# A transformer layer on eight cores: the layer norm's two stages and the attention's softmax closing in another order

## The chip, the cores and the metric

The kernel runs on one Trainium2 chip, on all 8 cores, each with one sequence of the batch (2048 tokens of 2048 features); the cores exchange nothing. The metric is the time of the slowest core in microseconds, as the median of several executions. TensorE is called PE, its weight loads PEld, VectorE DVE, ScalarE ACT, GpSimd POOL and SyncE SP, as in the profile.

## What is computed

The reference, cut to what matters, for the x of one core:

```python
def _layernorm(x, eps=1e-5):
    m = mean(x); v = var(x)
    return (x - m) / sqrt(v + eps)

# attention: 16 heads of 128
q, k, v = ln(x) @ wq, ln(x) @ wk, ln(x) @ wv
q, k = rope(q) / sqrt(128), rope(k)
probs = softmax(where(causal, q @ k.T, -1e30))
x = x + (probs @ v) @ wo

# experts: all 8 are computed, the gate keeps 2 per token, and 1 shared expert of twice the width
h = ln(x)
w = top2(softmax(h @ gate_w.T)), normalised
y = sum over experts e of w[e] * (silu(h @ w1[e]) * (h @ w3[e])) @ w2[e]
x = x + y + (silu(h @ sw1) * (h @ sw3)) @ sw2
```

## The kernel before

The program is one list of instructions per engine, written by a small class: `emit` appends an instruction to the list of its engine, with the semaphore values that it has to wait for and the semaphore that it raises. Each engine runs its list strictly in the order in which the Python code emitted it, so the order of the emitting lines is the order of the work. The stages follow one another and most begin behind a barrier:

1. First layer norm (lines 290 to 354), 16 tiles of 128 tokens. For each tile, SP loads 128x2048 float32 values of x into one of three buffers `xt`. `emit_ln` computes the statistics on ACT: a Copy whose accumulator gives the sum (line 292), and then a Square whose accumulator gives the sum of squares (line 295). Four tiny DVE instructions follow (mean, mean of squares plus eps, square of the mean, variance; lines 298 to 303), then Ln and Exp on ACT for the inverse root (lines 304 and 306), and the normalisation on DVE (line 308) into one of two bfloat16 buffers `sqb`. `emit_transposes` then turns the tile by 16 PE transposes into four groups of PSUM and copies the groups out on ACT (line 340). In the same stretch a long POOL DMA loads the whole of wk.
2. Projections of k, q and v with rope (lines 362 to 477), spilled to DRAM.
3. Attention (lines 530 to 642), 16 heads, each in two epochs of 1024 queries: the first epoch has 12 pieces of up to 512 queries against 128 keys, the second 28. For each piece PE makes the scores (line 575, into a PSUM slot), ACT takes the exponential (line 582), DVE masks it where the piece lies on the diagonal (line 589), and PE multiplies it twice: by a column of ones for the softmax sums Z (line 601, weights 128x1, into row 0 of the lower half of PSUM tensor `pB`) and by v for the output (line 609). The two multiplications come LA = 2 steps behind the scores. There are four score slots: two in the lower half of `pA`, and two in that upper half of `pA` or `pB` which the epoch's output does not use. When all pieces of an epoch are through, the epoch is closed: ACT copies Z out of PSUM (`zsb`, line 617), takes Ln and Exp(-x) of it (lines 620 and 622), PE spreads the reciprocal over 128 partitions by two matmuls with one row of weights (line 626), into the half that held slots 2 and 3, ACT copies that out (`bcs`, line 632), and DVE multiplies the output by it (`ATTNT`, line 636).
4. Output projection with the residual (lines 644 to 699).
5. Second layer norm with the gate (lines 708 to 796). The tile's layer norm is that of stage 1. 16 small matmuls (line 783) then give the gate's logits, which ACT copies out (line 790), and `gate_chain` (lines 725 to 768) computes the two weights per token: five tiny DVE instructions, two ACT exponentials (lines 737 and 740), seven more DVE instructions, one PE transpose (line 756), a DVE copy (line 761) and an SP store of the weights. `gate_chain` of a tile is emitted just ahead of the next tile's `emit_ln`.
6. The experts' first matrices (lines 840 to 910), with a spread of the next expert's gate weights at each expert's last block (`emit_gate_bcast`, line 831).
7. The experts' second matrices and the output (lines 925 to 1008).

What decides when a score may be written:

```python
sslot = step % 4
if sslot < 2: sps, soff, sw = pA, sslot * 512, [piece_free[sslot]]
else:         sps, soff, sw = bcps, 1024 + (sslot - 2) * 512, [piece_free[sslot], attn_free]
```

Of the kernel before, what the change touches and what calls it, by code (L numbers as in the profile page):

```python
# [10 lines left out]
AF = mybir.ActivationFunctionType  # L11
# [111 lines left out]
def build(taps=(), upto="p5b"):  # L123
# [126 lines left out]
    with contextlib.ExitStack() as stack:  # L250
# [40 lines left out]
        def emit_ln(xtile, dstb, src_toks, sq_waits=()):  # L291
            tcp = emit("scalar", lambda e: e.activation(dstb[:, :], xtile[:, :], AF.Copy,  # L292
                                                        accum_out=STATS[:, 0:1]),
                       waits=list(src_toks) + list(sq_waits), inc="s_s")
# [3 lines left out]
            vchain(lambda e: e.tensor_scalar_mul(STATS[:, 2:3], STATS[:, 0:1], 1.0 / D),  # L298
                   extra=[tsq])
            vchain(lambda e: e.tensor_scalar(STATS[:, 3:4], STATS[:, 1:2], 1.0 / D, EPS,  # L300
                                             ALU.mult, ALU.add))
            vchain(lambda e: e.tensor_mul(STATS[:, 4:5], STATS[:, 2:3], STATS[:, 2:3]))
            tv = vchain(lambda e: e.tensor_sub(STATS[:, 6:7], STATS[:, 3:4], STATS[:, 4:5]))
            tln = emit("scalar", lambda e: e.activation(STATS[:, 7:8], STATS[:, 6:7], AF.Ln),
                       waits=[tv], inc="s_s")
            tr = emit("scalar", lambda e: e.activation(STATS[:, 8:9], STATS[:, 7:8], AF.Exp,
                                                       scale=-0.5), waits=[tln], inc="s_s")
            emit("vector", lambda e: e.tensor_scalar(dstb[:, :], xtile[:, :], STATS[:, 2:3],  # L308
                                                     STATS[:, 8:9], ALU.subtract, ALU.mult),
# [38 lines left out]
        sq_free = [None, None]  # L348
        for i in range(NT):
# [180 lines left out]
        piece_free = {0: None, 1: None, 2: None, 3: None}  # L530
# [7 lines left out]
        for n in range(NH):  # L538
# [102 lines left out]
            if n + 2 < NH:  # L641
                hload[n + 2] = load_head(n + 2, [p.tokt("s_t")])
# [430 lines left out]
```

How the kernel before makes its waits and increments, by code:

```python
                def _(eng):  # L104
                    for fn, waits, incs in oplist:
                        for (s, v) in waits:
                            if v > 0 and lastwait.get(s, -1) < v:
                                eng.wait_ge(semh[s], v)
                                lastwait[s] = v
                        inst = fn(eng)
                        if inst is None:
                            assert not incs
                            continue
                        for (s, amt) in incs:
                            r = inst.then_inc(semh[s], amt)
                            if r is not None:
                                inst = r
```

## Time and profile before

| what | us |
|---|---|
| median of 4 timed executions | 7399.71 |
| the four: lowest, second, third, highest | 7374.02, 7380.34, 7419.08, 8093.21 |
| the profiled execution, its own time | 7080.52 |
| the profiled core's span (core 0, the slowest) | 7079.0 |
| spans of the eight cores | 7012.4 to 7079.0 |
| PE busy | 6255.1 (88%) |
| DVE busy | 1145.3 (16%) |
| ACT busy | 1048.2 (15%) |

| stage on core 0 | from | to |
|---|---|---|
| first layer norm | 0 | 186 |
| projections | 194 | 1018 |
| attention | 1037 | about 1800 |
| output projection | about 1800 | 2231 |
| second layer norm and gate | 2233 | 2450 |
| experts, first matrices | 2454 | about 5640 |
| experts, second matrices | about 5640 | 7079 |

The profile is one execution on the slowest core. A row of the timeline has the start and the duration, the engine, the line of the code, the operation, what is written from what, and in brackets how long the engine had been idle before it and what released it. "PEclk" is the share of TensorE's full clock that was granted. An engine that waits is not slow: what counts in a stage is which engine's chain the others wait for.

### The profile page before, as it was taken

Reading aid. Unit: us, or ns where it says so; the run is one execution under the profiler, and the core shown is the slowest. Engines: PE = TensorE matmul, PEld = TensorE weight load, DVE = VectorE, ACT = ScalarE, POOL = GpSimd, SP = SyncE. Lnnn points to the kernel's source line nnn. Section 1 sums busy time; section 2 is a strip of 40 time slices with the busy share of each in tenths; the row PEclk is TensorE's granted clock in tenths of the full one; section 3 lists DMA queues with packets and bytes.
Section 4 is the critical chain, followed back from the end, with each engine's and each line's share of the span. In section 5 each row is a group of like instructions: output and inputs, shape, how many; then the busy total and the mean of one; then the engine's idle time right before and its main releaser. Section 6 shows DMA issues by size and latency. Waiting matters only on the chain.

```text
span 7079.0 us, 66124 instructions; the slowest of 8 cores (7012.4 to 7079.0 us)
## 1 busy us (share of the span) xinstructions
PE 6255.1 (88%) x28144; PEld 2693.2 (38%) x28144; DVE 1145.3 (16%) x1337; ACT 1048.2 (15%) x1305; POOL 305.9 (4%) x280
## 2 busy tenths in 40 slices
PE   1778887777664399999999999999999999999999
PEld 1333331111222144444444444444444444444444
DVE  1222101111111211111111111111000122222222
ACT  5100116666101400000000000000000000000000
POOL 0000000000000000000000000000000000000000
PEclk9999997777887599999999999999999999999999
DMA  5133131010444144444444444444454544574544
GB/s 143 34 79 58 45 72 36 27 36 27 85 91 102 60 54 56 61 54 56 56 59 54 54 63 54 54 58 59 54 74 54 141 109 116 119 189 124 126 107 130
DMA packets 738001, 536.17 MB, mean 76 GB/s; under 512 B 531232, under 2 KB 652192, under 8 KB 733616
## 3 DMA queue, kind: packets, MB, share of 16 engines
q0 software_dynamic: 530896, 207.83, 25.4%
q1 hardware_dynamic: 92896, 208.76, 9.5%
q10 hardware_dynamic: 113920, 115.35, 5.1%
q8 instruction: 227, 3.72, 0.2%
q14 instruction: 62, 0.51, 0.0%
HBM read 623.18 MB, written 116.46 MB: 104 GB/s over the span
## 4 chain that ended last, share of the span: by engine, by line
PE 83%; DMA 7%; ACT 5%; DVE 3%; issue 2%; SPq 0%; DVEq 0%; ACTq 0%; POOL 0%; POOLq 0%
PE pB L879 22%; PE pA L864 21%; PE pA L975 11%; PE pB L975 10%; DMA xq<-xin 5%; PE pA L383 3%; PE pB L383 3%; PE pB L601 3%; PE pB L609 2%; PE pA L575 2%; PE pA L463 2%; PE pB L463 2%; DVE t2b L407 1%; ACT sqb L295 1%; ACT sqb L292 1%
## 5 line engine op out<-in xcount | busy, mean ns | idle before, releaser
L879 PE MATMUL pB<-XLNT,w3c 128*128 128x512 bf16 x7040 | 1555.1, 382 | 0.0
L864 PE MATMUL pA<-XLNT,w1c 128*128 128x512 bf16 x7040 | 1539.6, 379 | 2.1 <-ACT beb L837 2.1
L879 PEld LDWEIGHTS pB<-XLNT,w3c 128*128 128x128 bf16 x7040 | 692.1, 98 | 848.4 <-issue 29.0
L864 PEld LDWEIGHTS pA<-XLNT,w1c 128*128 128x128 bf16 x7040 | 689.8, 98 | 834.5 <-issue 6.0
L975 PE MATMUL pA<-w2s,aslg 128*128 128x512 bf16 x3520 | 788.6, 380 | 7.7 <-DMA AT_sp<-afin 5.3
L975 PE MATMUL pB<-w2s,aslg 128*128 128x512 bf16 x3520 | 785.8, 379 | 0.0
L871 ACT ACTIVATE silu<-pA 128x2048 bf16<-128x2048 f32 x110 | 206.5, 1877 | 2824.2 <-PE pA L864 2772.1
L892 DVE TENSOR_TENSOR atmp<-silu,pB 128x2048 bf16<-128x2048 bf16 x88 | 201.3, 2288 | 2165.2 <-PE pB L879 2140.9
L975 PEld LDWEIGHTS pA<-w2s,aslg 128*128 128x128 bf16 x3520 | 344.8, 98 | 426.0 <-issue 13.3
L975 PEld LDWEIGHTS pB<-w2s,aslg 128*128 128x128 bf16 x3520 | 344.4, 98 | 415.3
L582 ACT ACTIVATE exp<-pA,EXB 128x512 bf16<-128x512 f32 (+3 forms) x544 | 340.9, 640 | 146.9 <-PE pA L575 142.5
L677 PE MATMUL pA<-woq,ATTNT 128*128 128x512 bf16 x768 | 206.4, 432 | 110.8 <-DVE x2q L684 110.8
L575 PE MATMUL pA<-qtn,ktn 128*128 128x512 bf16 (+3 forms) x544 | 219.3, 415 | 48.7 <-DVE ATTNT L636 26.9
L994 DVE TENSOR_TENSOR Yacc<-Yacc,pB 128x1024 f32<-128x1024 f32 x144 | 175.9, 1222 | 508.9 <-PE pB L975 493.4
L994 DVE TENSOR_TENSOR Yacc<-Yacc,pA 128x1024 f32<-128x1024 f32 x144 | 175.9, 1222 | 508.2 <-PE pA L975 504.3
L329 PE MATMUL pA<-IDB,sqb 128*128 128x128 bf16 x256 | 32.4, 306 | 245.2 <-DVE sqb L308 245.2
L601 PE MATMUL pB<-exp,ONESC 128*1 128x512 bf16 (+3 forms) x640 | 239.7, 375 | 2.2 <-DVE exp L589 0.5
L518 POOL DMA_DIRECT2D w1c<-w x88 | 100.8, 1145 | 2231.1 <-PE pA L864 2231.1
L589 DVE TENSOR_TENSOR exp<-exp,TRIUB 128x128 bf16<-128x128 bf16 x256 | 57.6, 225 | 712.2 <-ACT exp L582 712.2
L609 PE MATMUL pB<-exp,vn 128*128 128x512 bf16 (+1 forms) x448 | 172.5, 385 | 0.0
L677 PEld LDWEIGHTS pA<-woq,ATTNT 128*128 128x128 bf16 x768 | 80.5, 108 | 236.5 <-issue 175.3
L383 PE MATMUL pA<-XLNT,qc 128*128 128x512 bf16 x512 | 120.5, 399 | 43.0 <-DMA qc<-wq 24.4
(119 smaller groups left out, 2721.9 us busy)
## 6 DMA issues: line engine op xcount, KB each, us to landing
aslg<-AT_sp ACTq DMA_DIRECT2D x80, 1408.0 KB, 8.2
AT_sp<-afin SPq DMA_DIRECT2D x110, 512.0 KB, 7.9
w1c<-w POOLq DMA_DIRECT2D x88, 512.0 KB, 6.7
w3c<-w POOLq DMA_DIRECT2D x88, 512.0 KB, 10.8
w2s<-w POOLq DMA_DIRECT2D x16, 2816.0 KB, 22.9
xt<-xin SPq DMA_DIRECT2D x16, 1024.0 KB, 8.3
xq<-xin SPq DMA_DIRECT2D x64, 256.0 KB, 5.1
X_sp<-x2q SPq DMA_DIRECT2D x64, 256.0 KB, 3.8
```

Of the source, the lines that this page charges most:

```text
L383: lhs_tile=lhs_tile: e.matmul(ps[:, c * 512:(c + 1) * 512], lhs_tile[:, lcol:lcol + 128], XLNT[:, db * 2048 + c * 512: db * 2048 + (c + 1) ...
L463: emit("tensor", lambda e, db=db, c=c, ps=ps, i=i: e.matmul(ps[:, c * 512:(c + 1) * 512], XLNT[:, db * 2048 + i * 128: db * 2048 + (i + 1) ...
L575: sps=sps, soff=soff: e.matmul(sps[:, soff:soff + b - a], ktn[par][:, j * 128:(j + 1) * 128], qtn[par][:, q0 + a:q0 + b], start=True, stop ...
L582: sps=sps, soff=soff: e.activation(expt[my_epar][:, 0:b - a], sps[:, soff:soff + b - a], AF.Exp, bias=EXB[:, 0:1]),
L601: stz=first_z[bank], gsp=grp_stop: e.matmul(pB[0:1, a:b], ONESC[:, :], expt[my_epar][:, 0:b - a], start=stz, stop=gsp),
L609: gsp=grp_stop, atps=atps: e.matmul(atps[:, 1024 + a:1024 + b], vn[par][:, j * 128:(j + 1) * 128], expt[my_epar][:, 0:b - a], start=stt, s ...
L677: emit("tensor", lambda e, nb=nb, i=i, pcol=pcol, wbuf=wbuf: e.matmul(pA[:, pcol:pcol + 512], ATTNT[:, nb * 2048 + i * 128: nb * 2048 + (i ...
L864: emit("tensor", lambda e, db=db, c=c, slot=slot: e.matmul(pA[:, c * 512:(c + 1) * 512], w1c[slot][:, db * 128:(db + 1) * 128], XLNT[:, db ...
L871: tsilu = emit("scalar", lambda e: e.activation(silu[:, :], pA[:, :], AF.Silu), waits=[th, silu_free], inc="s_s")
L879: emit("tensor", lambda e, db=db, c=c, slot=slot: e.matmul(pB[:, c * 512:(c + 1) * 512], w3c[slot][:, db * 128:(db + 1) * 128], XLNT[:, db ...
L975: ap2=cur_ap2, psl=psl: e.matmul(psl[0][:, psl[1] + c * 512: psl[1] + (c + 1) * 512], aslg[ap2][:, ib * 512 + kk * 128: ib * 512 + (kk + 1 ...
L994: tac = emit("vector", lambda e, k=k, psl=psl: e.tensor_add(Yacc[k][:, :], Yacc[k][:, :], psl[0][:, psl[1]:psl[1] + 1024]), waits=[tmm, ya ...
```

## The change

Three things are edited.

The layer norm is cut into `ln_stats` and `ln_rest`. The sum is now a `reduce_sum` on DVE over the float32 tile, the Copy on ACT is gone, and the Square stays on ACT. Statistics of tile i are emitted behind all the work of tile i-1 (its `ln_rest`, its transposes and its copies out), and `ln_rest` of tile i comes in the next turn of the loop. Two sets of columns of `STATS` alternate. The loads are emitted two tiles ahead. Both layer norms use this; in the second one, `gate_chain` of tile i-1 is now emitted behind the statistics of tile i and ahead of its `ln_rest`.

In the attention, the closing of an epoch is moved into `emit_zchain`, which is emitted at the start of the next epoch. The copy `zsb` is gone: Ln reads Z from PSUM itself. The scores have two slots, both in `pA`, and the two multiplications come LA = 3 steps behind.

```diff
+        def ln_stats(xtile, dstb, src_toks, sq_waits, C):
+            tsq = emit("scalar", lambda e: e.activation(dstb[:, :], xtile[:, :], AF.Square,
+                                                        accum_out=c1(C[1])),
                        waits=list(src_toks) + list(sq_waits), inc="s_s")
-            tsq = emit("scalar", lambda e: e.activation(dstb[:, :], xtile[:, :], AF.Square,
-                                                        accum_out=STATS[:, 1:2]),
-                       waits=[tcp], inc="s_s")
...
+            tsum = vchain(lambda e: e.reduce_sum(c1(C[0]), xtile[:, :], axis=AX.X),
+                          extra=list(src_toks))
+            return tsq, tsum
+
+        def ln_rest(xtile, dstb, tsq, tsum, C):
+            vchain(lambda e: e.tensor_scalar_mul(c1(C[2]), c1(C[0]), 1.0 / D),
+                   extra=[tsum])
+            vchain(lambda e: e.tensor_scalar(c1(C[3]), c1(C[1]), 1.0 / D, EPS,
+                                             ALU.mult, ALU.add), extra=[tsq])
...
+        def ln_finish(pend):
+            nonlocal ev_prev
+            j, jpar, jbpar, jst = pend
+            tx = ln_rest(xt[jpar], sqb[jbpar], *jst, LNCOLS[j % 2])
+            xt_free[jpar] = tx
+            ev_prev, sq_free[jbpar] = emit_transposes(j, ev_prev, tx, sqb[jbpar])
+
+        lts_q = {0: load_xt(0, 0, xin), 1: load_xt(1, 1, xin)}
         for i in range(NT):
             par = i % 3
             bpar = i % 2
-            lts = load_xt(i, par, xin)
-            tx = emit_ln(xt[par], sqb[bpar], lts, sq_waits=[sq_free[bpar]])
-            xt_free[par] = tx
-            ev_prev, sq_free[bpar] = emit_transposes(i, ev_prev, tx, sqb[bpar])
+            if pend_ln is not None:
+                ln_finish(pend_ln)
+            if i + 2 < NT:
+                lts_q[i + 2] = load_xt(i + 2, (i + 2) % 3, xin)
+            st = ln_stats(xt[par], sqb[bpar], lts_q[i], [sq_free[bpar]], LNCOLS[i % 2])
+            pend_ln = (i, par, bpar, st)
+        ln_finish(pend_ln)
...
+        LA = 3
+
+        def emit_zchain(st):
...
+            tlnz = emit("scalar", lambda e: e.activation(recf[:, :], pB[0:1, 0:1024],
+                                                         AF.Ln),
+                        waits=[st["tlast"]], inc="s_s")
...
+                if pend_z is not None:
+                    emit_zchain(pend_z)
+                    pend_z = None
...
-                        sslot = step % 4
-                        if sslot < 2:
-                            sps, soff = pA, sslot * 512
-                            sw = [piece_free[sslot]]
-                        else:
-                            sps, soff = bcps, 1024 + (sslot - 2) * 512
-                            sw = [piece_free[sslot], attn_free]
+                        sslot = step % 2
+                        sps, soff = pA, sslot * 512
...
-                            waits=([bc_free] if first_attn[bank] else []),
+                            waits=([tbcs_done[(epoch + 1) % 2]]
+                                   if first_attn[bank] else []),
...
-                tz = emit("scalar", lambda e: e.activation(zsb[:, :], pB[0:1, 0:1024], AF.Copy),
-                          waits=[tlast], inc="s_s")
-                z_free = tz
-                tlnz = emit("scalar", lambda e: e.activation(recf[:, :], zsb[:, :], AF.Ln),
-                            waits=[tz], inc="s_s")
...
+        def p3b_finish(pend):
...
+            if pending is not None:
+                gate_chain(*pending)
+                pending = None
+            tx = ln_rest(xt[jpar], sqb[jbpar], *jst, LNCOLS[j % 2])
```

DVE's list in the second layer norm, before: a tile's normalisation (L308), then the gate chain of that tile (L727 to L761), then the first two small instructions of the next tile's statistics.

```order
L308 TENSOR_SCALAR sqb_54<-xt_51,STATS 128x2048 [waits s_s]
L727 TENSOR_REDUCE STATS<-STATS 128x1 [waits s_v,s_s]
...
L735 TENSOR_TENSOR STATS<-STATS 128x1 [waits s_v]
L742 TENSOR_SCALAR STATS<-STATS 128x2 [waits s_v,s_s]
...
L761 COPY gt_58<-pB 8x128 [waits s_t]
L298 TENSOR_SCALAR STATS<-STATS 128x1 [waits s_v,s_s]
L300 TENSOR_SCALAR STATS<-STATS 128x1 [waits s_v]
```

The same place after the change, from one tile's normalisation (L315) to the next: the sum (L300), the gate chain (L754 to L788) and the rest of the layer norm (L305 to L315).

```order
L315 TENSOR_SCALAR sqb_55<-xt_52,STATS 128x2048 [waits s_s]
L300 TENSOR_REDUCE STATS<-xt_53 128x1 [waits s_v,l_xt2]
L754 TENSOR_REDUCE STATS<-STATS 128x1 [waits s_v,s_s]
...
L762 TENSOR_TENSOR STATS<-STATS 128x1 [waits s_v]
L769 TENSOR_SCALAR STATS<-STATS 128x2 [waits s_v,s_s]
...
L788 COPY gt_58<-pB 8x128 [waits s_t,st_gsp]
L305 TENSOR_SCALAR STATS<-STATS 128x1 [waits s_v]
L307 TENSOR_SCALAR STATS<-STATS 128x1 [waits s_v]
```

The sum of the next tile has moved in ahead of the gate chain, and the four small instructions of the layer norm, whose first one waited for ACT, now stand behind it without such a wait.

PE's list at the boundary of two epochs, before: the last multiplication by v (L609), the two spreading matmuls (L626), the scores of the next epoch (L575), its Z (L601) and output (L609).

```order
L609 MATMUL pB<-exp_80,vn_75 128x128
L626 MATMUL pA<-recb,ONESR 128x512 [waits s_s]
L626 MATMUL pA<-recb,ONESR 128x512
L575 MATMUL pA<-qtn_72,ktn_74 128x512 [waits l_h1]
L575 MATMUL pA<-qtn_72,ktn_74 128x512
L575 MATMUL pB<-qtn_72,ktn_74 128x384 [waits s_v]
L601 MATMUL pB<-exp_77,ONESC 1x512 [waits s_v]
L609 MATMUL pA<-exp_77,vn_76 128x512 [waits s_s]
L575 MATMUL pB<-qtn_72,ktn_74 128x512
L601 MATMUL pB<-exp_78,ONESC 1x512 [waits s_s]
```

The same boundary after the change, with the lines 655 (times v), 573 (spread), 621 (scores) and 647 (Z):

```order
L655 MATMUL pB<-exp_80,vn_75 128x128
L573 MATMUL pA<-recb,ONESR 128x512 [waits l_h1,s_s]
L573 MATMUL pA<-recb,ONESR 128x512
L621 MATMUL pA<-qtn_72,ktn_74 128x512 x2
L621 MATMUL pA<-qtn_72,ktn_74 128x384 [waits s_s]
L621 MATMUL pA<-qtn_72,ktn_74 128x512 [waits s_s]
L647 MATMUL pB<-exp_77,ONESC 1x512 [waits s_v]
L655 MATMUL pA<-exp_77,vn_76 128x512
L621 MATMUL pA<-qtn_72,ktn_74 128x256 [waits s_s]
L647 MATMUL pB<-exp_78,ONESC 1x512
```

The two spreading matmuls keep their place between the epochs. The third score waits for ACT instead of DVE, a fourth score stands ahead of the first Z, and from then on the wait for ACT stands at each score where it stood at each Z.

## Rows read from the trace of the kernel before

**Rows 1.** Windows view: us, busy (count) of PE, PEld, DVE, ACT, POOL, PEclk, DMA.
```profile
1018.00:1797.00 779.00, 593.98 (x1982) 134.61 (x1982) 94.31 (x287) 517.84 (x766) 5.72 (x5) 0.78 0.16 39
```

**Rows 2.** Timeline, one tile of the first layer norm, up to the next tile's Copy.
```profile
33.38 1.94 ACT L292 ACTIVATE sqb<-xt 128x2048 bf16<-128x2048 f32 x1
...
35.51 1.91 ACT L295 ACTIVATE sqb<-xt 128x2048 bf16<-128x2048 f32 x1
...
37.61 0.15 DVE L298 TENSOR_SCALAR STATS<-STATS 128x1 f32<-128x1 f32 x1 [6.97 <-ACT sqb L295]
37.87 0.15 DVE L300 TENSOR_SCALAR STATS<-STATS 128x1 f32<-128x1 f32 x1
...
39.25 1.35 DVE L308 TENSOR_SCALAR sqb<-xt,STATS 128x2048 bf16<-128x2048 f32 x1 [0.70 <-ACT STATS L306]
...
43.45 1.94 ACT L292 ACTIVATE sqb<-xt 128x2048 bf16<-128x2048 f32 x1
```

**Rows 3.** Groups by line: DVE's slowest 128x2048 instruction, busy us, mean ns.
```profile
L407 DVE TENSOR_TENSOR t2b<-pA,SSINB 128x2048 bf16<-128x2048 f32 x16 | 36.7, 2292 | 199.2 <-PE pA L399 199.2
```

**Rows 4.** DMA view of 35 to 45 us: the load of x issued there, us to landing.
```profile
xt<-xin SPq DMA_DIRECT2D x1, 1024.0 KB, 11.1
```

**Rows 5.** Timeline, one boundary of two epochs of the attention.
```profile
1096.15 1.01 ACT L617 ACTIVATE zsb<-pB 1x1024 f32<-1x1024 f32 x1 [0.95 <-PE pA L609]
1097.26 1.05 ACT L620 ACTIVATE recf<-zsb 1x1024 f32<-1x1024 f32 x1
1098.40 1.05 ACT L622 ACTIVATE recb<-recf 1x1024 bf16<-1x1024 f32 x1
...
1099.60 1.01 PE L626 MATMUL pB<-recb,ONESR 1*128 1x512 bf16 x2 [3.55 <-ACT recb L622]
...
1100.54 1.03 PE L575 MATMUL pA<-qtn,ktn 128*128 128x512 bf16 x2
...
1101.68 1.26 ACT L582 ACTIVATE exp<-pA,EXB 128x512 bf16<-128x512 f32 x2
...
1103.26 0.58 PE L575 MATMUL pA<-qtn,ktn 128*128 128x512 bf16 x1 [1.68 <-DVE ATTNT L636]
```

**Rows 6.** Timeline, one step in the middle of an epoch.
```profile
1108.40 0.38 PE L575 MATMUL pA<-qtn,ktn 128*128 128x512 bf16 x1
...
1108.88 0.69 ACT L582 ACTIVATE exp<-pA,EXB 128x512 bf16<-128x512 f32 x1 [0.16 <-PE pA L575]
...
1109.25 0.38 PE L575 MATMUL pA<-qtn,ktn 128*128 128x512 bf16 x1
```

**Rows 7.** Windows view, granted clock behind the third score of Rows 5.
```profile
1103.30:1107.40 4.10, 4.10 (x9) 0.66 (x10) 0.00 (x0) 1.88 (x3) 0.00 (x0) 0.50 0.00 0
1107.50:1111.00 3.50, 3.50 (x14) 0.77 (x12) 0.00 (x0) 2.58 (x5) 0.00 (x0) 1.00 0.00 0
```

**Rows 8.** Timeline, second layer norm, from one copy of the logits to the next.
```profile
2249.24 0.17 ACT L790 COPY STATS<-pB 128x8 f32<-128x8 f32 x1 [0.91 <-PE pB L783]
...
2250.90 0.20 ACT L737 ACTIVATE STATS<-STATS 128x1 f32<-128x1 f32 x1 [1.50 <-DVE STATS L735]
...
2251.50 0.17 DVE L742 TENSOR_SCALAR STATS<-STATS 128x2 f32<-128x2 f32 x1 [0.69 <-ACT STATS L740]
...
2254.12 0.28 DVE L761 COPY gt<-pB 8x128 f32<-8x128 f32 x1 [0.62 <-PE pB L756]
...
2257.13 1.34 DVE L308 TENSOR_SCALAR sqb<-xt,STATS 128x2048 bf16<-128x2048 f32 x1 [0.70 <-ACT STATS L306]
...
2262.26 0.17 ACT L790 COPY STATS<-pB 128x8 f32<-128x8 f32 x1 [0.91 <-PE pB L783]
```

**Rows 9.** Timeline, experts' first matrices, the end of the first expert.
```profile
2736.52 13.98 PE L864 MATMUL pA<-XLNT,w1c 128*128 128x512 bf16 x64
...
2752.67 1.86 PE L831 MATMUL pA<-gr,ONESR 1*128 1x512 bf16 x4 [2.17 <-ACT silu L871]
...
2754.46 16.46 PE L879 MATMUL pB<-XLNT,w3c 128*128 128x512 bf16 x64
```

More of the change, by code:

```diff
@@ L768, in gate_chain @@
             gsp_toks.append(tsp)
+        def p3b_finish(pend):
+            nonlocal ev_prev, gate_free, pending
+            j, jpar, jbpar, jst = pend
+            if pending is not None:
+                gate_chain(*pending)
+                pending = None
+            tx = ln_rest(xt[jpar], sqb[jbpar], *jst, LNCOLS[j % 2])
+            xt_free[jpar] = tx
+            ev_prev, sq_free[jbpar] = emit_transposes(j, ev_prev, tx, sqb[jbpar])
+            tev_all = ev_prev[3]
+            for db in range(ND):
+                emit("tensor", lambda e, db=db, j=j: e.matmul(
+                    pB[:, 0:8],
+                    XLNT[:, db * 2048 + j * 128: db * 2048 + (j + 1) * 128],
+                    GWTB[:, db * 8:(db + 1) * 8],
+                    start=(db == 0), stop=(db == ND - 1)),
+                    waits=[tev_all, gate_free], inc="s_t")
+            tg = p.tokt("s_t")
+            tgl = emit("scalar", lambda e, jbpar=jbpar: e.copy(
+                STATS[:, 48 + 8 * jbpar: 56 + 8 * jbpar], pB[:, 0:8]),
+                waits=[tg, chain_done[jbpar]], inc="s_s")
+            gate_free = tgl
+            pending = (j, jbpar, tgl)
+        p.phase(BAR3)
+        lts_q = {0: load_xt(0, 0, X2_sp), 1: load_xt(1, 1, X2_sp)}
         for i in range(NT):
@@ L773, in build @@
             p.phase(BAR3)
-            lts = load_xt(i, par, X2_sp)
-            if pending is not None:
-                gate_chain(*pending)
-                pending = None
-            tx = emit_ln(xt[par], sqb[bpar], lts, sq_waits=[sq_free[bpar]])
-            xt_free[par] = tx
-            ev_prev, sq_free[bpar] = emit_transposes(i, ev_prev, tx, sqb[bpar])
-            tev_all = ev_prev[3]
-            for db in range(ND):
-                emit("tensor", lambda e, db=db, i=i: e.matmul(
-                    pB[:, 0:8],
-                    XLNT[:, db * 2048 + i * 128: db * 2048 + (i + 1) * 128],
-                    GWTB[:, db * 8:(db + 1) * 8],
-                    start=(db == 0), stop=(db == ND - 1)),
-                    waits=[tev_all, gate_free], inc="s_t")
-            tg = p.tokt("s_t")
-            tgl = emit("scalar", lambda e, bpar=bpar: e.copy(
-                STATS[:, 48 + 8 * bpar: 56 + 8 * bpar], pB[:, 0:8]),
-                waits=[tg, chain_done[bpar]], inc="s_s")
-            gate_free = tgl
-            pending = (i, bpar, tgl)
+            if pend_ln is not None:
+                p3b_finish(pend_ln)
+            if i + 2 < NT:
+                lts_q[i + 2] = load_xt(i + 2, (i + 2) % 3, X2_sp)
+            st = ln_stats(xt[par], sqb[bpar], lts_q[i], [sq_free[bpar]], LNCOLS[i % 2])
+            pend_ln = (i, par, bpar, st)
+        p3b_finish(pend_ln)
+        pend_ln = None
         gate_chain(*pending)
```

80 lines of the change are left out of this document (42 added, 38 removed).

## The prediction

> **What bounds the kernel now.** I read the busy times of the page first: PE is busy for 88% of the span, and the two expert stages, two thirds of it, are dense matmuls that the change does not touch. So I went to the stages that it does touch, with the windows view for their totals and the timeline for one period of each. In all three the reader is to see a chain over several engines in which PE or ACT waits in turn.
>
> In the first layer norm one tile takes 10.07 us, from Copy to Copy (33.38 to 43.45) [rows 2]. Copy and Square follow each other on ACT, DVE's small steps wait for them, the normalisation for those, the transposes for it, and the next Copy stands behind the copies out. Nothing overlaps between tiles. The load of x is no part of the chain: it landed in 11.1 us while the wk transfer ran [rows 4], with three buffers, thus two tiles ahead.
>
> In the attention PE is busy for 594 of 779 us at a mean clock of 0.78 [rows 1]. A full step takes 0.85 us, and ACT is idle 0.16 us in it, waiting for PE [rows 6]: PE's own order is the limit, not the exponential. The loss is at the 31 boundaries between epochs: PE stands 3.55 us until the reciprocal is there, and 1.68 us more ahead of the third score, which waits for DVE's ATTNT [rows 5]. Behind that the clock is at 0.50, the 1.2 GHz level, until 1107.4, and then at 1.00 [rows 7].
>
> In the second layer norm a tile takes 13.02 us, from one copy of the logits to the next (2249.24 to 2262.26) [rows 8]: the same chain plus the gate.
>
> **First layer norm.** Removed: the Copy with the sum, 33.38 to 35.51, so 2.13 us of ACT per tile [rows 2]. Added: one float32 reduction of 128x2048 on DVE, which the trace does not show. The nearest rows are the normalisation, the same tile read once by DVE, at 1.35 us [rows 2], and DVE's slowest instruction of that size, 2.29 us [rows 3]. I take 2.29, since a reduction is not faster than a plain pass. For its path that choice does not matter: it stands directly behind the normalisation of the tile before, which ends at 40.60, and would end by 42.9, while ACT is at the copies out and starts the Square only where the Copy started, at 43.45. Its cover goes if it takes more than about 4.5 us. The mean then is also ready before the Square, so 0.26 us (L298 to L300) leaves the path. New period: 10.07 - 2.13 - 0.26 = 7.68 us, 2.39 less; over the 15 tiles behind the first 35.9 us. The first tile has nothing ahead of it: its sum runs beside the Square, and instead of 4.23 us (33.38 to 37.61) it takes at most 2.29 plus a hop of 0.11, 1.8 less. Together 37.7 us. The loads keep their distance: tile i's is still released by the normalisation of tile i-3 and needed at that of i-1, two periods later, 15.4 us against 11.1. What is late next is what was late before, the barrier behind the last copy out and the load of the cosine tables; wk landed long before (80 us).
>
> **Attention.** Emitting the closing at the head of the next epoch moves nothing by itself: PE's list has the two spreading matmuls between the same neighbours as before, and no score of the next epoch ahead of them. So the boundary stays, only shorter. First, the copy zsb goes: 1097.26 - 1096.15 = 1.11 us [rows 5], in all 32 closings, 35.5 us. Ln has to read PSUM now; I cost that at nothing, as both kinds of 1x1024 ACT instruction take 1.01 to 1.05 us [rows 5]. Second, the third score has a slot in pA and waits for the first exponential instead of ATTNT. That exponential starts at 1101.68 and takes 0.69 [rows 6]; with the hop of 0.15 from ACT to PE (1098.40 + 1.05 to 1099.60) the score could start at 1102.52 instead of 1103.26, 0.74 earlier. The fourth score now stands ahead of the first Z and waits for the second exponential: both together end at 1101.68 + 1.26 = 1102.94, with the hop 1103.09. The third score occupies PE for 0.43 us at that clock (512 columns at 1.2 GHz), to 1102.95, so 0.14 of the gain goes again. Left: 0.60 us at 31 boundaries, 18.6 us. LA = 3 is costed at nothing: PE's amount of work is the same, and Z does not wait for exponentials in the middle of an epoch now.
>
> The new waits: each score waits for the exponential two steps back, where it was four. Behind that wait stand the Z and output matmuls of the step, and ACT waits for the score. A slot turns around in 0.48 (score to exponential, 1108.40 to 1108.88) + 0.69 + 0.15 = 1.32 us, against two steps of 0.85, 1.70 [rows 6]. The slack is 0.38 us: no cost. Attention together 54.1 us. Its bounds: the copy alone, with every microsecond of it worth half (below), 18, and 54 plus the clock's whole price, 131.
>
> **Second layer norm.** Here the order of DVE matters. Before, the gate chain of tile i-1 had its second half under the Copy and Square of tile i. Now it stands ahead of the small steps of tile i, and its two exponentials stand on ACT behind the Square. The new period, step by step, starting at the copy of the logits: 0.17 for it, then the Square 2.13 (as from one ACT pass to the next [rows 2]); during it the gate's first five DVE steps run, 1.66 us (2249.24 to 2250.90), hidden. Then the exponentials, 0.60 (2250.90 to 2251.50), the seven DVE steps, PE's transpose and DVE's copy, 2.62 (to 2254.12), that copy and a hop, 0.39, the small steps up to the normalisation, 1.64 (37.61 to 39.25 [rows 2]), and from there to the next copy of the logits 5.13 (2257.13 to 2262.26). Sum 12.68, against 13.02: the Copy's 2.1 us and the first half of the gate are bought with the second half of the gate. 0.34 over 15 tiles is 5.1, and 1.8 for the first tile as above: 6.9 us. Here the layer norm's stages gain alike in work and not at all alike in time. The bounds: 0, and 15 times 2.39 plus 1.8, so 38, if nothing of the gate came onto the path.
>
> **Sum.** 37.7 + 54.1 + 6.9 = 98.7 us. The span of 7079.0 becomes 6980, the profiled execution's 7080.5 becomes 6982. The timed median is 7399.7, 4.5% above the profiled execution, and the profile does not show why. The three stages are bound by fixed times of ACT, DVE and hops, so I subtract the same microseconds: 7301.
>
> **The rivals.**
>
> The slow clock keeps its end. Below the boundary PE works at half rate until 1107.4 [rows 7]. If that moment does not come earlier with PE's work, what is moved forward only fills the slow stretch and gains half: 1.71 / 2 at 31 boundaries plus 1.1, 28 us in place of 54. For it: the clock is granted by what PE does, and the first part of the gain is only an earlier start of four matmuls. Against: PE works without a gap for the 4.1 us before the clock is back, and that gapless work starts earlier by the whole 1.71. Total 73 us, 7327.
>
> The clock does not fall. PE's idle time shrinks from 3.55 to 2.44 us. A drop of the clock costs 16.46 - 13.98 = 2.48 us, as in the 64 matmuls behind the gate's spread [rows 9], so without it 31 times 2.48, 77 us more: 7224. Against: in that same place the idle time was only 2.17 us, shorter than the 2.44, and the clock fell.
> The Trainium skill, "TensorE: Matmul & The Clock Gate", section "Why this matters for your kernels", advises to keep the idle gaps between bursts of matmuls short, and its limit would let the shortened gap pass. By that rule this rival would be the forecast; the trace does not agree, with its fall behind 2.17 us, and I go by the trace.
>
> The loads of x hold the pace. Under the wk transfer they came every 10.07 us because nobody asked for more. If they cannot come faster there, the first 8 tiles gain nothing: 8 x 2.39 = 19 us less, 7320. Against: they landed in 11.1 us, and two are allowed to be under way.
>
> Slower: the two score slots. If PE's wait at each score also keeps it from loading the weights ahead, each of the 640 scores pays the hop of 0.15 and a weight load, 134.61 / 1982 = 0.07 us [rows 1]: 0.22 x 640 = 141 us, 42 more than all gains, 7442. It decides from 98.7 / 640 = 0.15 us per score. For it: the wait moves from Z, where it was, to the score, whose weights are loaded under the matmul before. Against: the slack of 0.38 us per pair of steps, so the wait is over when PE comes to it.
>
> The boundary stays as it is. If the closing took as long as before, because Ln from PSUM is slow by the microsecond of the copy, 35 us would go: 7337. The rows speak against it.
>
> **How the numbers follow.** Forecast 0.52, with a range of its own of 7285 to 7317. The clock keeping its end 0.19, the loads 0.08, the closing staying 0.05, the two slots 0.04, the clock not falling 0.05, and 0.07 for part of that gain at some boundaries (about 7270). The range reaches to the cases on both sides, and the timed runs themselves scatter by 20 us around their median: 7258 to 7356. One per cent is 74 us, about what a measurement of this kernel can tell from no change. Faster by over 1%: the forecast, the clock's two good cases and a little more than a fourth of the others, 0.71. Within 1%: 0.25. Slower: 0.04.
>
> **What would show it.** Right: a tile of the first layer norm in about 7.7 us with DVE's sum beginning at the normalisation's end and ending before the Square; ACT's Ln 0.3 us behind the last matmul of an epoch, PE idle about 2.4 us there and about 0.9 us ahead of the third score; steps of 0.85 us in the middle; two epochs together shorter by 2 x 1.71 = 3.4 us; a tile of the second layer norm in about 12.7 us with the gate's second half on DVE behind the Square. Wrong: a middle step longer than 0.85 us, with PE waiting for ACT at the scores; two epochs shorter by less than 2 us; ACT waiting for xt in the first 90 us; or a clock of 1.00 across a boundary.

## The result, and the profile after

The changed kernel's timed executions had a median of 7270.95 us (6976.45 to 7918.31), those of the kernel before 8023.58 (7374.02 to 8113.29; ten executions, among them the four of the table further up). The plain ratio of the two medians is 0.906. The forecast was 7301 us, a ratio of 0.987. In most executions of either kernel the cores of one die, or of both, are granted a lower clock, down to 0.82 in place of 0.95, and the result's own ratio, 0.868 (0.850 to 0.885), is meant to leave these out, but none of the ten of before took less than 7374 us, where its profiled execution took 7080.52, so 0.868 is not the change's doing alone. The profiled executions, with all eight cores at 0.94 to 0.96 in both kernels, stand at 7080.52 and 6976.45 us, 104.07 apart, a ratio of 0.985; the forecast had 6982 for the second.

The stages as the median of the eight cores (us). Each begins with its first matmul in the trace and ends with the next one's; the first layer norm begins with the span, and the second with the last addition to x (`x2q`):

| stage | before | after | difference | forecast |
|---|---|---|---|---|
| first layer norm | 195.6 | 158.0 | -37.6 | -37.7 |
| projections | 847.0 | 847.0 | 0 | 0 |
| attention | 766.5 | 710.2 | -56.3 | -54.1 |
| output projection | 398.5 | 405.1 | +6.6 | 0 |
| second layer norm | 229.5 | 219.0 | -10.5 | -6.9 |
| experts, first matrices | 3073.7 | 3071.2 | -2.5 | 0 |
| experts, second matrices | 1536.5 | 1539.7 | +3.2 | 0 |

The output projection lies between 356 and 445 us from core to core over the kernels of this study, so its 6.6 us can't be told from that scatter. The three edited stages gave 104.4 us.

**First layer norm**, the timeline of after, core 0, one tile from its normalisation to the next. It answers to [rows 2]:

```profile
42.49 1.35 DVE L315 TENSOR_SCALAR sqb<-xt,STATS 128x2048 bf16<-128x2048 f32 x1 [0.70 <-ACT STATS L313]
44.01 2.29 DVE L300 TENSOR_REDUCE STATS<-xt 128x1 f32<-128x2048 f32 x1 [0.17 <-DVE sqb L315]
...
45.73 1.09 ACT L347 COPY XLNT<-pB 128x512 bf16<-128x512 bf16 x2
46.40 0.15 DVE L305 TENSOR_SCALAR STATS<-STATS 128x1 f32<-128x1 f32 x1
46.68 1.94 ACT L297 ACTIVATE sqb<-xt 128x2048 bf16<-128x2048 f32 x1
...
48.82 0.15 DVE L307 TENSOR_SCALAR STATS<-STATS 128x1 f32<-128x1 f32 x1 [2.26 <-ACT sqb L297]
...
50.20 1.34 DVE L315 TENSOR_SCALAR sqb<-xt,STATS 128x2048 bf16<-128x2048 f32 x1 [0.70 <-ACT STATS L313]
```

The reader is to see three things. The period is 50.20 - 42.49 = 7.71 us. The sum, 2.29 us, begins 0.17 behind the normalisation and is over at 46.30, before the Square begins. And DVE then waits 2.26 us for the Square at L307, so the sum has room.

**Attention**, the timeline of after, core 0, an epoch boundary. It answers to [rows 5]:

```profile
1094.78 0.23 PE L655 MATMUL pB<-exp,vn 128*128 128x128 bf16 x1
1095.11 1.01 ACT L565 ACTIVATE recf<-pB 1x1024 f32<-1x1024 f32 x1 [1.51 <-PE pB L655]
1096.21 1.05 ACT L568 ACTIVATE recb<-recf 1x1024 bf16<-1x1024 f32 x1
1097.41 0.84 PE L573 MATMUL pA<-recb,ONESR 1*128 1x512 bf16 x2 [2.40 <-ACT recb L568]
1098.18 1.03 PE L621 MATMUL pA<-qtn,ktn 128*128 128x512 bf16 x2
1098.40 1.02 ACT L578 ACTIVATE bcs<-pA 128x1024 bf16<-128x1024 f32 x1 [1.13 <-PE pA L573]
1099.32 2.77 ACT L628 ACTIVATE exp<-pA,EXB 128x512 bf16<-128x512 f32 x4
1100.14 1.16 PE L621 MATMUL pA<-qtn,ktn 128*128 128x384 bf16 x2 [0.93 <-ACT exp L628]
1101.23 0.58 PE L647 MATMUL pB<-exp,ONESC 128*1 128x512 bf16 x1
...
1122.97 0.69 ACT L628 ACTIVATE exp<-pA,EXB 128x512 bf16<-128x512 f32 x1 [0.16 <-PE pA L621]
1123.82 0.69 ACT L628 ACTIVATE exp<-pA,EXB 128x512 bf16<-128x512 f32 x1 [0.16 <-PE pA L621]
```

Ln from PSUM takes 1.01 us, as the copy from PSUM did; from SBUF Ln took 1.05. PE is idle 2.40 us where it was 3.55, and 0.93 where it was 1.68. A step in the middle is still 0.85 us long (the last two lines). The windows view of after, core 0: the whole attention (it answers to [rows 1]), a stretch that begins at the boundary above, and one behind it (they answer to [rows 7]); the columns are those of [rows 1], the granted clock being the third number from the end:

```profile
1010.00:1720.00 710.00, 592.64 (x1984) 141.97 (x1984) 95.30 (x288) 481.48 (x736) 0.00 (x0) 0.84 0.15 37
1097.50:1104.10 6.60, 5.57 (x13) 0.83 (x12) 1.81 (x4) 3.92 (x6) 0.00 (x0) 0.51 0.59 173
1104.80:1109.80 5.00, 5.00 (x22) 1.60 (x21) 1.12 (x5) 3.03 (x7) 0.00 (x0) 1.00 0.00 0
```

PE is busy for nearly what it was, 592.6 us against 595.0, but the mean clock rose from 0.78 to 0.84. Behind this boundary the clock stands at its lower level, 1.2 GHz, up to about 1104.4. In the trace of before, core 0, the same stage has a stretch of 10.2 us at 0.50 at each of its 31 boundaries, 317 us in all; after has 27 of 6.8 us, three of 10.2 and one of 3.4, 218 us in all. The prediction did not contain that. In PE's busy time it shows only as those 2.4 us, since what the stretch lost is mostly its part in PE's idle time: in the mean of the 31 boundaries it began 2.3 us ahead of the spread and now begins 0.8 us behind the spread's start, and it ends 7.9 and 7.8 us behind it.

**Second layer norm**, the timeline of after, core 0, from one copy of the logits to the next. It answers to [rows 8]:

```profile
2158.83 0.17 ACT L815 COPY STATS<-pB 128x8 f32<-128x8 f32 x1 [0.92 <-PE pB L808]
2158.91 1.91 ACT L297 ACTIVATE sqb<-xt 128x2048 bf16<-128x2048 f32 x1
...
2160.82 0.19 ACT L764 ACTIVATE STATS<-STATS 128x1 f32<-128x1 f32 x1
...
2161.41 0.17 DVE L769 TENSOR_SCALAR STATS<-STATS 128x2 f32<-128x2 f32 x1 [1.01 <-ACT STATS L767]
...
2164.45 0.28 DVE L788 COPY gt<-pB 8x128 f32<-8x128 f32 x1 [0.69 <-PE pB L783]
2164.84 0.15 DVE L305 TENSOR_SCALAR STATS<-STATS 128x1 f32<-128x1 f32 x1
...
2166.47 1.35 DVE L315 TENSOR_SCALAR sqb<-xt,STATS 128x2048 bf16<-128x2048 f32 x1 [0.70 <-ACT STATS L313]
...
2171.61 0.17 ACT L815 COPY STATS<-pB 128x8 f32<-128x8 f32 x1 [0.92 <-PE pB L808]
```

This tile takes 12.78 us; five of the 15 periods do, ten take 12.43, and their mean went from 13.05 to 12.55. The gate's second half (2161.41 to 2164.73) stands openly between the Square and the layer norm's own small steps.

### The profile page after: what moved, and what is told of

It reads as the page before. It is cut to its first block, busy times and chain, and to the rows that moved or that the text cites. A ratio compares the mean times of both kernels' runs of the same rounds, so it can differ in the third digit from the quotient of the medians.

```text
span 6974.9 us, 66198 instructions; the slowest of 8 cores (6900.4 to 6974.9 us)
## 1 busy us (share of the span) xinstructions
PE 6240.1 (89%) x28144; PEld 2696.7 (39%) x28144; DVE 1218.4 (17%) x1369; ACT 944.2 (14%) x1209; POOL 305.9 (4%) x280
## 4 chain that ended last, share of the span: by engine, by line
PE 84%; DMA 7%; ACT 3%; DVE 3%; issue 2%; SPq 0%; DVEq 0%; POOL 0%; ACTq 0%; POOLq 0%
PE pB L919 22%; PE pA L904 22%; PE pA L1015 11%; PE pB L1015 10%; DMA xq<-xin 4%; PE pA L404 3%; PE pB L404 3%; PE pB L647 3%; PE pA L621 2%; PE pB L655 2%; PE pA L484 2%; PE pB L484 2%; DMA aslg<-AT_sp 1%; DVE t2b L428 1%; PE pA L655 1%
## 5 line engine op out<-in xcount | busy, mean ns | idle before, releaser
L628 ACT ACTIVATE exp<-pA,EXB 128x512 bf16<-128x512 f32 (+3 forms) x640 | 386.5, 622 | 161.8 <-PE pA L621 149.9
L621 PE MATMUL pA<-qtn,ktn 128*128 128x512 bf16 (+3 forms) x640 | 255.8, 409 | 62.3 <-ACT exp L628 35.2
L704 PEld LDWEIGHTS pA<-woq,ATTNT 128*128 128x128 bf16 x768 | 77.4, 104 | 215.6 <-issue 147.7
```

Of the source, the lines that this page charges most:

```text
L621: sps=sps, soff=soff: e.matmul(sps[:, soff:soff + b - a], ktn[par][:, j * 128:(j + 1) * 128], qtn[par][:, q0 + a:q0 + b], start=True, stop ...
L628: sps=sps, soff=soff: e.activation(expt[my_epar][:, 0:b - a], sps[:, soff:soff + b - a], AF.Exp, bias=EXB[:, 0:1]),
L704: emit("tensor", lambda e, nb=nb, i=i, pcol=pcol, wbuf=wbuf: e.matmul(pA[:, pcol:pcol + 512], ATTNT[:, nb * 2048 + i * 128: nb * 2048 + (i ...
```

## The experiments

Three theories stood against one another for the attention. Additive: each microsecond taken off a boundary is a microsecond of the stage, so the copy is worth 1.11 us at 32 closings and the third score 0.60 at 31. Clock: the stretch at the low clock changes with the boundary, so the parts are not additive. And, for the whole, that 0.868 is the code's.

**The kernel before without the copy zsb.**

```diff
-                tz = emit("scalar", lambda e: e.activation(zsb[:, :], pB[0:1, 0:1024], AF.Copy),
-                          waits=[tlast], inc="s_s")
-                z_free = tz
-                tlnz = emit("scalar", lambda e: e.activation(recf[:, :], zsb[:, :], AF.Ln),
-                            waits=[tz], inc="s_s")
+                tlnz = emit("scalar", lambda e: e.activation(recf[:, :], pB[0:1, 0:1024],
+                                                             AF.Ln),
+                            waits=[tlast], inc="s_s")
+                z_free = tlnz
```

> The kernel before, with one edit: Ln reads the softmax sums from PSUM itself and the copy zsb is gone; four score slots, LA = 2 and the order of the closing stay. Theory A (every microsecond at a boundary is worth itself): the attention, 766 us on the median core, takes 32 x 1.11 = 35.5 us less, 731. Theory B (PE's slow stretch behind a boundary is as long as PE's idle time makes it, so parts of a boundary are not additive): between 18 and 36 us less, I expect 28, and slow stretches of 10.25 us that have partly become shorter. Theory C (Ln from PSUM is slow by what the copy took): 766, Ln at 2 us. The layer norms stay at 10.07 and 13.05 us per tile.

Measured: attention 737.6 us against 766.5. The copy alone is worth 28.9 us and not 35.5, so the additive theory fails already here.

**The changed kernel with the copy put back.**

```diff
-            tlnz = emit("scalar", lambda e: e.activation(recf[:, :], pB[0:1, 0:1024],
-                                                         AF.Ln),
-                        waits=[st["tlast"]], inc="s_s")
+            tz = emit("scalar", lambda e: e.activation(zsb[:, :], pB[0:1, 0:1024], AF.Copy),
+                      waits=[st["tlast"]], inc="s_s")
+            tlnz = emit("scalar", lambda e: e.activation(recf[:, :], zsb[:, :], AF.Ln),
+                        waits=[tz], inc="s_s")
```

> The changed kernel with the copy zsb put back ahead of Ln, nothing else. Theory A: the attention goes from 710 us to 710 + 35 = 745. Theory B: with PE idle 3.5 us again at each boundary the slow stretches of the clock are as long as in the kernel before, 10.25 us, and the 0.6 us won at the third score by two slots and LA = 3 are lost in them: the attention takes 760 to 767, as before the change. The layer norm's stages stay at 158 and 219 us.

Measured: attention 766.2 us, the time of before. The whole 56 us are gone, though only the copy came back, and the third score is as early as in after. PE's timeline in this kernel, core 0, at a boundary:

```profile
1102.04 0.23 PE L656 MATMUL pB<-exp,vn 128*128 128x128 bf16 x1
1105.81 1.01 PE L574 MATMUL pA<-recb,ONESR 1*128 1x512 bf16 x2 [3.55 <-ACT recb L569]
1106.75 1.03 PE L622 MATMUL pA<-qtn,ktn 128*128 128x512 bf16 x2
1108.72 1.16 PE L622 MATMUL pA<-qtn,ktn 128*128 128x384 bf16 x2 [0.93 <-ACT exp L629]
```

The first gap is that of before, 3.55, and the second that of after, 0.93. The windows view of the same kernel, behind that boundary, further on, and the whole stage:

```profile
1105.00:1114.70 9.70, 7.86 (x18) 1.30 (x18) 2.03 (x5) 5.64 (x9) 0.00 (x0) 0.50 0.42 116
1115.00:1120.00 5.00, 4.45 (x21) 1.56 (x20) 0.90 (x4) 3.08 (x6) 0.00 (x0) 1.00 0.00 0
```
```profile
1011.60:1778.90 767.30, 619.59 (x1985) 142.56 (x1986) 95.26 (x288) 515.71 (x768) 0.00 (x0) 0.78 0.14 34
```

All 31 stretches at the low clock are 10.2 us long again. The same view for the whole attention of before and of the kernel without the copy, core 0:

```profile
1037.13:1803.10 765.97, 594.98 (x1984) 134.74 (x1985) 95.53 (x288) 520.86 (x768) 0.00 (x0) 0.79 0.14 34
1037.06:1774.44 737.38, 599.75 (x1984) 134.89 (x1985) 95.41 (x288) 486.83 (x736) 0.00 (x0) 0.81 0.15 35
```

Split into PE's busy and idle time, with the place where the low clock ends, counted from the start of the spread (mean of the 31 boundaries), all in us on core 0:

| kernel | attention | PE busy | PE idle | low clock ends at |
|---|---|---|---|---|
| before | 766.0 | 595.0 | 171.0 | 7.9 |
| before without the copy | 737.4 | 599.8 | 137.6 | 8.7 |
| changed, copy put back | 767.3 | 619.6 | 147.7 | 9.1 |
| changed | 709.6 | 592.6 | 117.0 | 7.8 |

PE's idle time nearly adds up: 33.4 us less by the one edit, 23.3 by the other, 54.0 by both. Its busy time does not: 4.8 and 24.6 us more with either edit alone, 2.4 less with both. With one edit alone the low clock ends later behind the spread, so more matmuls run at half rate; with the copy put back that eats the whole gain, and two epochs take 47.8 us, as before. So the third score is worth nothing beside the copy (766.5 to 766.2), and 27.4 us without it (737.6 to 710.2). "The third score" stands here for all that the change does to the attention besides the copy: the early score, the two slots and LA = 3 came together, and only LA is taken alone, in the next experiment.

**The changed kernel with LA = 2.**

```diff
-        LA = 3
+        LA = 2
```

> The changed kernel with LA = 2 for LA = 3, so that the first Z stands ahead of the fourth score again. I costed LA = 3 at nothing: the attention stays at 710 within 4 us. Rival: with two score slots the third step of distance is what keeps PE from waiting for the exponential; then each of the 640 steps loses something, and already 0.05 us each would be 32 us.

Measured: 712.9 us against 710.2. The prediction costed the third step of distance at nothing; it is worth at most 2.7 us, and two traces of the changed kernel itself differ by 1.7 (710.2 and 711.9).

**The changed kernel with the spread of the reciprocal behind the second score.** Ln and Exp stay at the head of the epoch, the two spreading matmuls, the copy `bcs` and the multiplication go behind step 1. PE then has two scores to do while ACT works on the reciprocal.

```diff
+            st["trecb"] = trecb
+
+        def emit_zspread(st):
...
+                    if step == 1 and pend_z is not None:
+                        emit_zspread(pend_z)
+                        pend_z = None
```

> The changed kernel with the two spreading matmuls, the copy bcs and the multiplication emitted behind the second step of the next epoch instead of ahead of its first: PE makes the first two scores while ACT takes Ln and Exp, and ACT takes the first two exponentials ahead of bcs. This is the overlap that the change itself does not reach. Theory A: the third score no longer waits for bcs and an exponential (PE idle 0.93 us there, and 0.86 us of scores move into the 2.40 us of idle time ahead of the spread), the output of the first step waits for bcs instead; 1.3 to 1.8 us per boundary, 40 to 56 us less attention, 655 to 670. Theory B: more than that, since the slow stretches shorten too, 645 to 655. Rival: the first output matmul's wait for bcs takes the place of what is won, 700 or more.

Measured: attention 659.7 us, 50.5 less than after; the profiled execution took 6939.09. The timeline of this kernel, core 0, at a boundary:

```profile
1088.11 0.23 PE L663 MATMUL pA<-exp,vn 128*128 128x128 bf16 x1
1088.18 0.59 PE L626 MATMUL pA<-qtn,ktn 128*128 128x512 bf16 x2
1088.44 1.01 ACT L565 ACTIVATE recf<-pB 1x1024 f32<-1x1024 f32 x1 [1.51 <-PE pA L663]
1089.54 1.05 ACT L568 ACTIVATE recb<-recf 1x1024 bf16<-1x1024 f32 x1
1090.50 1.23 ACT L633 ACTIVATE exp<-pA,EXB 128x512 bf16<-128x512 f32 x2
1090.74 1.01 PE L579 MATMUL pB<-recb,ONESR 1*128 1x512 bf16 x2 [1.97 <-ACT recb L568]
1091.68 1.03 PE L626 MATMUL pA<-qtn,ktn 128*128 128x512 bf16 x2
1092.64 0.58 PE L655 MATMUL pB<-exp,ONESC 128*1 128x512 bf16 x1
```

The two scores fill a part of the first gap, now 1.97 us, and the exponentials of the new epoch start before the spread, so the second gap, ahead of the third score, is gone. Two epochs take 40.9 us against 44.3. The windows view behind the boundary shows that the clock fell all the same:

```profile
1090.50:1096.60 6.10, 5.86 (x13) 1.04 (x13) 1.22 (x1) 4.79 (x8) 0.00 (x0) 0.50 0.00 0
1097.80:1103.00 5.20, 5.20 (x20) 1.16 (x18) 0.00 (x0) 4.19 (x7) 0.00 (x0) 1.00 0.01 3
```

**The layer norms' part alone, and the attention's alone.** The first is the kernel before with `ln_stats`, `ln_rest`, the new loops of both layer norms and the loads ahead, the second the kernel before with `emit_zchain`, two slots and LA = 3. Of each the line that tells it:

```diff
+            st = ln_stats(xt[par], sqb[bpar], lts_q[i], [sq_free[bpar]], LNCOLS[i % 2])
```
```diff
+                if pend_z is not None:
+                    emit_zchain(pend_z)
+                    pend_z = None
```

> The kernel before with the changed layer norms alone (ln_stats, ln_rest, loads two tiles ahead, gate chain behind the statistics); the attention as before. Theory A (the stages are independent): first layer norm 158 us in place of 195.6, second 219 in place of 229.5, attention 766, together 48 us less than before, 7051 to 7003 on the median core, a ratio of 0.993. Theory B (the clock or a DMA carries part of it on): another attention or projection time, by over 5 us. Rival for the large measured ratio of the whole change: if 0.87 were true of the code, this half or the other would show hundreds of microseconds in one stage; I expect none.

> The kernel before with the changed attention alone; the layer norms as before. Theory A: attention 710 us in place of 766, layer norms 195.6 and 229.5: 56 us less, a ratio of 0.992. With ln_only it should add up to the whole change, 104 us of the median core's 7051, 0.985.

Measured: the ratio to before is 0.9937 (0.9915 to 0.9960) for the layer norms and 0.9921 (0.9897 to 0.9946) for the attention. Together 1.4% faster, about what the whole is by its profile. The stages are those of after to 1.2 us: 158.7 and 220.2 us for the layer norms, 710.0 for the attention. The attention of the first is 766.8 us and the layer norms of the second are 196.5 and 228.7, as before to 0.9. No effect of layer norm and attention on each other shows.

**The changed kernel once more**, with no edit, for the ratio.

> The changed kernel itself once more, timed in alternation with the kernel before on one chip. Theory A: the stages of the profile are all that the change does: 0.985, between 0.983 and 0.988, when undisturbed executions are compared. Theory B: the ratio of 0.868 is the code's; then it comes again here, and the profile of a kernel before that took 8000 us must show where 900 us more than in its first profile are.

Measured: 0.9866 (0.9826 to 0.9906), though the plain medians of that comparison are 7822.91 for after and 7212.03 for before. This agrees with the profiles' 0.985 and with the forecast's 0.987, and not with 0.868.

**Both gaps that were left: the spread behind the second score, and the gate's chain cut in three.** The gate's first five DVE steps come behind the normalisation, its exponentials behind the copies of the transposes, the second half behind the statistics of the tile after.

```diff
-        def gate_chain(i, par, tgl):
+        def gate_head(i, par, tgl):
...
+            t_d = gate_head(*pending) if pending is not None else None
...
+                gtail = (pending[0], pending[1], gate_exps(t_d))
...
+                gate_tail(*gtail)
```

> The changed kernel with the spread behind the second step (as zspread) and with the gate chain cut: its first five DVE steps directly behind the tile's normalisation, its two exponentials on ACT behind the copies out, its seven further steps, transpose and copy behind the next tile's sum, where DVE is idle while ACT takes the Square. The gate then leaves the path: a tile of the second layer norm takes 5.13 + 0.17 + 2.13 + 1.38 = 8.8 us in place of 12.55, 56 us less over 15 tiles, the stage 163 us in place of 219. Rival: DVE has the sum (2.29), both halves of the gate (1.4 + 2.3) and 2.5 us of the layer norm in one period, and the second half ends behind the Square; then 9.5 us per tile or more. Attention 660. In all 7051 - 104 - 50 - 56 = 6840 on the median core, a ratio of 0.970.

> The same kernel as best (the changed kernel with the spread of the reciprocal moved behind the second score, and the gate's chain cut), for its ratio to the kernel before, in more rounds. Stages of the median core as in best: 659 us attention and 186 us second layer norm. From the profiled executions (6911.95 against 7080.52 us own time) the ratio should be 0.976, between 0.970 and 0.981; the forecast made for best before, 0.970, rested on a second layer norm of 163 us, which it did not have.

Measured: own time of the profiled execution 6911.95 us, and from the second set of executions a ratio of 0.9728 (0.9704 to 0.9753) to the kernel before. It beats both kernels. Attention 659.0 us, as alone; the second layer norm 185.7, not the 163 expected. Its timeline, core 0, between two tiles' first transposes (2132.11 and 2142.21, a tile of 10.10 us):

```profile
2132.11 1.01 PE L336 MATMUL pA<-IDB,sqb 128*128 128x128 bf16 x8 [5.26 <-DVE sqb L315]
...
2133.55 2.29 DVE L300 TENSOR_REDUCE STATS<-xt 128x1 f32<-128x2048 f32 x1 [0.17 <-DVE STATS L770]
...
2135.84 1.91 ACT L297 ACTIVATE sqb<-xt 128x2048 bf16<-128x2048 f32 x1
2136.01 0.17 DVE L784 TENSOR_SCALAR STATS<-STATS 128x2 f32<-128x2 f32 x1 [0.18 <-ACT STATS L833]
...
2138.63 0.28 DVE L803 COPY gt<-pB 8x128 f32<-8x128 f32 x1 [0.62 <-PE pB L798]
2139.01 0.15 DVE L305 TENSOR_SCALAR STATS<-STATS 128x1 f32<-128x1 f32 x1
```

The gate's first half now keeps DVE's sum back to 2133.55, and the second half starts only behind that sum and needs until 2138.91, 1.06 us longer than the Square and the read of its accumulator, an instruction of its own (to 2137.85). The cut hides most of the gate, not all of it.

**DVE's sum doubled**, in both layer norms. The second result goes over the first.

```diff
+            tsum = vchain(lambda e: e.reduce_sum(c1(C[0]), xtile[:, :], axis=AX.X),
+                          extra=list(src_toks))
```

> The changed kernel with DVE's sum over a tile (2.29 us, 128x2048) issued twice in both layer norms, the second result over the first. If the sum lies free beside the transposes and copies, as the prediction has it (the sum begins 0.17 us behind the normalisation, and its result is wanted only when ACT's Square ends some 6 us later), the first layer norm stays at 158 us of the median core (157 to 160) and the second at 219 (218 to 223, since its logits come some 5 us behind the normalisation and a second sum ends 4.8 us behind it). If the sum has a share in the tile's length, each of 16 tiles is longer by up to 2.4 us: 196 and 257 us.

Measured over the eight cores: first layer norm 164.2 to 167.1 us, second 229.5 to 232.3. Neither expectation holds: each tile is dearer, but not by the whole sum. The timeline, core 0, first layer norm:

```profile
74.28 2.29 DVE L302 TENSOR_REDUCE STATS<-xt 128x1 f32<-128x2048 f32 x1
74.56 1.94 ACT L297 ACTIVATE sqb<-xt 128x2048 bf16<-128x2048 f32 x1
76.37 0.22 ACT L297 ACTIVATION_READ_ACCUMULATOR sqb<-xt 128x1 f32 x1
76.67 0.15 DVE L307 TENSOR_SCALAR STATS<-STATS 128x1 f32<-128x1 f32 x1
77.00 0.15 DVE L309 TENSOR_SCALAR STATS<-STATS 128x1 f32<-128x1 f32 x1 [0.18 <-DVE STATS L307]
```

The second sum ends at 76.57 and the Square with its accumulator's read at 76.59, at the same time. The mean (L307 here) that was ready ahead of the Square now stands behind it: a tile takes 8.01 us (the normalisations at 62.36 and 70.37), 0.30 more, which over 15 tiles is 4.5, and the first tile, where nothing hides it, pays a further 2.29: together 6.8, against 6.5 measured on core 0 (165.1 and 158.6). The prediction had said that the sum's cover goes at about 4.5 us; two sums are 4.6, and there it goes. In the second layer norm a tile takes 13.14 us in place of 12.55.

## Why the prediction was right, and where it was wrong

**The terms.** First layer norm: 7.68 us a tile against 7.71, and 37.7 against 37.6. The loads of x did not hold the pace: the mean of the 15 periods on core 0 is 7.75 us, where it was 10.14. The choice of 2.29 us for the sum, the upper of two rows, was the value measured. The cover's limit was confirmed by the doubled sum.

Attention: idle times of 2.44 and 0.9 us were predicted, 2.40 and 0.93 measured; two epochs shorter by 3.4 us, measured 3.5 in the mean of core 0; steps of 0.85; Ln from PSUM and the two slots cost nothing that shows. The sum was 54.1 against 56.3, and PE's idle time on core 0 fell by 54.0. But its steps, "1.11 us in all 32 closings, 35.5 us" and "0.60 us at 31 boundaries, 18.6 us", are not true one by one. The copy alone gives 28.9, the third score alone 0.3, the two together 56.3, so 27 us come only from both. What is wrong there is that every microsecond of a gap counts in full, for which the low clock's end has to move with PE's work and PE's busy time to stay what it is. That holds with both edits (2.4 us less) and not with either alone (4.8 and 24.6 us more). Nothing in the working told these cases apart, so that the sum came out within 2.2 us is in part luck.
The rival "the slow clock keeps its end" would have given half of each gain. With both edits it fell: the end moved with PE's work (7.9 and 7.8 us behind the spread). Alone, the copy kept more than half, 28.9 of 35.5, and the third score nearly nothing, 0.3 of 18.6, so neither the forecast nor that rival describes a single edit. The rival "the clock does not fall" fell too: there is a stretch at the lower level at every boundary of every kernel.
The Trainium skill, "TensorE: Matmul & The Clock Gate", section "Why this matters for your kernels", would let gaps of 2.40 and 1.97 us pass; the clock fell here at both, so the trace does not agree, and keeping to its limit would not have kept the clock.

Second layer norm: 6.9 against 10.5. The 15 periods gave 15 x (13.05 - 12.55) = 7.5 us where 5.1 was forecast: the step "Sum 12.68" stands against a mean of 12.55, and the 13.02 of before against 13.05. The mis-sized term is the way from the copy of the logits to the first exponential, 0.17 + 2.13 = 2.30 in the prediction and 1.99 in the trace (2158.83 to 2160.82): the 2.13 holds the read of the accumulator, and the exponential starts already as the Square ends. Against it, the gate's second half up to the copy `gt` takes 2.69 us in ten tiles and 3.04 in five, where 2.62 was taken; why it is longer in every third tile is open. From the first tile's pass over xt to its copy of the logits it was 10.98 us and is 9.25, 1.7 less, as forecast (1.8). Behind the last copy of the logits the stage ends 1.0 us sooner, which the sum did not have and which I did not follow up; the first load costs what it did (8.3 and 8.1 us).

**The forecast's failed step** is the base: "The timed median is 7399.7, 4.5% above the profiled execution, and the profile does not show why. ... so I subtract the same microseconds: 7301." It takes for fixed a distance of 319 us that is not the kernel's. The distance belongs to the executions: the same kernel before had medians of 7399.7, 8023.6, 7212.0 and 7287.0 us, and after 7271.0 and 7822.9 (the four executions of the first median are among the ten of the second). Where such a distance sits can be read in the kernel with the doubled sum, whose cores differ within one execution: the experts' second matrices take 1538 us on core 0, at a granted clock of 0.99, and 1808 on core 4, at 0.83, while the second layer norm takes 229.5 and 230.6. It is added in dense matmuls that the change does not touch. So that after's 7271.0 lay within the range, 7258 to 7356, is luck (the repeat had 7822.9), and the ratio to before as measured beside it, 0.868, lay far outside what the range stood for, 0.981 to 0.994. The range of a ratio by the cases was right (0.985 by the profiles, 0.9866 by the repeat); what it left out is the scatter of the base, larger than every term of the sum. The prediction's own remark, that the profile did not show why the median stood 4.5% higher, was the place at which to widen. So was the fourth of the times that it had: "the timed runs themselves scatter by 20 us around their median" holds for three of them, and the fourth, 8093.21, stands 693 us above.

## What to carry to other kernels

Where PE's granted clock falls at every boundary of a loop, the parts of an edit at that boundary can't be priced one by one: take them away singly and together, and read PE's busy time beside its idle time, since one gap shortened can be paid back in matmuls at half rate. An in-order engine's work is hidden only up to the next instruction behind it: behind the first tile the second sum itself stayed hidden but put a 0.15 us step behind the Square, for 0.30 us a tile, and the cut gate was held up by the sum that it had itself moved. When a timed median stands some per cent above the profiled execution and no row says why, the time may belong to the execution and not to the kernel. Then forecast the ratio from the profile and widen the time's range for the base.

## What was not expected of the hardware

The low-clock stretches of one kernel's attention have few lengths (core 0): 10.2 us at all 31 boundaries before and with the copy put back, 16 of 6.8 and 15 of 10.2 without the copy, 27 of 6.8, three of 10.2 and one of 3.4 in after, 29 of 6.8 and two of 3.4 with the spread moved. The same edit, the third score's, was so worth nothing beside the copy and 27.4 / 31 = 0.88 us at a boundary without it, more than the 0.75 by which the gap shrank. With the copy in place, two epochs take 47.78 us before and 47.79 with the third score's edit (means of core 0), equal to 0.01 us although the gaps differ by 0.75 at each boundary: the period looks held by something else than PE's gaps, and the fixed place of the low clock in each period (it begins 2.3 us ahead of the spread in the one kernel, 1.2 in the other) points to the clock. What sets the choice between the lengths is not shown by these runs.
